# Attention plan of a four-layer decoder: accumulators turned, normalised and put out one step sooner, and x turned closer behind its norm

## The reference, cut to what matters

```
xn  = layernorm(x)
q   = (xn @ Wq + bq) * 8 ** -0.5      # k, v from xn (causal) or from the context (cross)
p   = softmax(q @ k.T + mask/ALiBi)   # 16 heads, 256 x 256
x   = x + (p @ v per head) @ Wo + bo
```

## Time and profile before

| | |
|---|---|
| time, median of 3 runs | 1073.76 us (1073.03 to 1091.79) |
| profiled execution, own time | 1073.34 us |
| its span, first to last instruction | 1071.5 us |
| mean granted TensorE clock | 0.868 of full speed |
| PE, PEld busy | 810.3 us (76%), 590.2 us (55%) |
| DVE, ACT, POOL busy | 613.3 (57%), 349.4 (33%), 316.3 us (30%) |
| the attention of layer 0 in the trace | about 98 to 178 us |
| the attentions of layer 2, the later part beside them | about 448 to 640 us |

### The profile page before, as it was taken

How to read it: one execution, slowest core, us unless ns; L and a number is a source line. 1 busy time by engine, 2 the same in 40 slices (tenths; PEclk the granted TensorE clock), 3 DMA queues, 4 the chain that set the end, 5 groups by cost and what they waited for, 6 DMA issues and landing times. The chain is left out here.

```text
span 1071.5 us, 15970 instructions
## 1 busy us (share of the span) xinstructions
PE 810.3 (76%) x5961; PEld 590.2 (55%) x5969; DVE 613.3 (57%) x1423; ACT 349.4 (33%) x684; POOL 316.3 (30%) x318
## 2 busy tenths in 40 slices
PE   6865896982687285688887747999999995177994
PEld 3632453581354183577654425577877785045994
DVE  4554862323669973885767698663364447742222
ACT  0210574330121112155555623543342331011331
POOL 3263100203238734232222111000251624415232
PEclk9985898896687687899989788999999998558998
DMA  9402200361000005344562000000000000006684
GB/s 362 168 2 87 74 5 1 109 189 27 20 1 1 0 1 106 82 109 87 155 183 60 3 0 1 2 2 2 1 2 2 2 1 1 1 3 211 218 282 145
DMA packets 44966, 72.44 MB, mean 68 GB/s; under 512 B 4849, under 2 KB 37025, under 8 KB 43321
## 3 DMA queue, kind: packets, MB, share of 16 engines
q1 hardware_dynamic: 38921, 65.52, 20.7%
q0 software_dynamic: 1728, 3.59, 1.0%
q10 hardware_dynamic: 4240, 2.30, 0.8%
HBM read 58.65 MB, written 15.89 MB: 70 GB/s over the span
## 5 line engine op out<-in xcount | busy, mean ns | idle before, releaser
L863 DVE TENSOR_REDUCE space<-PS 128x2 f32<-128x512 f32 x128 | 83.8, 686 | 29.3 <-PE PS L667 28.8
L2580 DVE TENSOR_REDUCE space<-PS 128x2 f32<-128x512 f32 x64 | 43.3, 689 | 83.0 <-PE PS L2278 82.8
L847 ACT ACTIVATE annex<-PS 128x384 f32<-128x384 f32 (+1 forms) x128 | 67.2, 544 | 48.5 <-PE PS L678 21.8
L2315 PEld LDWEIGHTS PS<-space 128*128 128x128 f32 x512 | 61.2, 191 | 16.8 <-issue 16.5
L2315 PE MATMUL PS<-space 128*128 128x65 f32 x512 | 68.6, 280 | 0.0
L2295 PE MATMUL PS<-space 64*128 64x256 f32 x256 | 67.0, 402 | 0.2 <-ACT space L2398 0.2
L1982 POOL TENSOR_TENSOR space<-space 128x1536 f32<-128x1536 f32 x16 | 54.6, 3439 | 32.7 <-ACT space L1840 26.4
L2278 PE MATMUL PS<-space 64*128 64x256 f32 x256 | 62.7, 400 | 0.1
L1186 PE MATMUL PS<-space 128*128 128x128 f32 x444 | 55.3, 278 | 6.0 <-ACT space L1255 2.4
L2627 POOL TENSOR_SCALAR var_eps<-moments 128x2 f32<-128x2 f32 x16 | 3.5, 220 | 185.2 <-DVE moments L2409 185.2
L1321 DVE TENSOR_TENSOR space<-PS,space 128x512 f32<-128x512 f32 (+1 forms) x28 | 19.2, 686 | 67.1 <-ACT space L1248 61.9
(11 more groups left out here) (492 smaller groups left out, 2182.8 us busy)
## 6 DMA issues: line engine op xcount, KB each, us to landing
space<-in_e_l_ffn SPq DMA_DIRECT2D x22, 768.0 KB
space<-in_e_l_ffn SPq DMA_DIRECT2D x23, 192.0 KB, 2.6
l_ffn_sorted<-in_slots SPq DMA_DIRECT2D x2, 1584.0 KB, 24.8
space<-l_attn_scratch_k SPq DMA_DIRECT2D x8, 384.0 KB
space<-l_ffn_sorted SPq DMA_DIRECT2D x10, 264.0 KB, 4.2
weights<-in_w_l_xattn SPq DMA_DIRECT2D x1, 2504.0 KB, 13.7
weights<-in_w_l_attn SPq DMA_DIRECT2D x1, 2124.0 KB, 11.8
space<-l_xattn_scratch_q SPq DMA_DIRECT2D x4, 512.0 KB, 3.5
```

The lines of the kernel that those rows point to most:

```text
L847: nc.scalar.activation(P[:, u % 8, 0:keys], PS[:, 3 + u % 2, 0:keys], ACT.Exp).then_inc(exp_done, 1)
L863: nc.vector.tensor_reduce(m[:, :, at_h], max_bank(u).rearrange("p (c k) -> p c k", c=2), AX_X, ALU.max).then_inc(max_done, 1)
L2315: last = nc.tensor.matmul(out, p[:, 256 * kc + 128 * qc:256 * kc + 128 * qc + 128], VB[:, b % 2, kc, h, :], start=kc == 0, stop=kc == 1)
L2580: nc.vector.tensor_reduce(MX[:, b % 2, :, h], PS[:, max_bank[a], :].rearrange("p (c k) -> p c k", c=2), AX_X, ALU.max).then_inc(max_done, 1)
```

## The change

The turn B, the normalisation, the turn E and the output O each move one step ahead. The statistics of x for passes n >= 4 are tied to `out_at`, and so move one step ahead too, and XN with them. The turn of XN moves from two steps behind XN to one step behind for those passes (`lag` is 2 there), and the query with it, so T and Q move two steps. For n < 4 `lag` is 3, and T and Q stay where they are (2 x 3 - 1 = 3 + 2). The copy (L840), K, V and M keep their steps. No instruction is added or removed.

```
--- before.py
+++ after.py
@@ -603,8 +603,8 @@
     done_at = lambda n: second_at(16 * n + 15)
     four_at = {second_at(4 * j + 3) + 2: j for j in range(U // 4)}
     copy_at = {second_at(8 * v + 7) + 3: v for v in range(U // 8)}
-    norm_at = {second_at(8 * v + 7) + 6: v for v in range(U // 8)}
-    out_at = lambda n: done_at(n) + 9
+    norm_at = {second_at(8 * v + 7) + 5: v for v in range(U // 8)}
+    out_at = lambda n: done_at(n) + 8
 
     def norm1_at(n):
         return 9 * n - 20 if n < 2 else first_at(n) - 24 if n < 4 else out_at(n - 4) + 1
@@ -614,8 +614,8 @@
     stats_at, xn_at = {norm1_at(n): n for n in range(N)}, {norm1_at(n) + lag(n): n for n in range(N)}
     jobs = []
     for n in range(N):
-        jobs.append((norm1_at(n) + lag(n) + 2, "T", n))
-        jobs.append((norm1_at(n) + lag(n) + 4, "Q", n))
+        jobs.append((norm1_at(n) + 2 * lag(n) - 1, "T", n))
+        jobs.append((norm1_at(n) + 2 * lag(n) + 1, "Q", n))
         if kind(n) == "causal":
             jobs.append((norm1_at(n) + 6, "K", n))
             jobs.append((norm1_at(n) + 8, "V", n))
@@ -626,7 +626,7 @@
         jobs.append((out_at(n) - 1, "E", n))
         jobs.append((out_at(n), "O", n))
     for v in range(U // 8):
-        jobs.append((second_at(8 * v + 7) + 5, "B", v))
+        jobs.append((second_at(8 * v + 7) + 4, "B", v))
     jobs.sort()
     max_at = {first_at(n) + 19: n for n in range(N)}
     assert all(a[0] < b[0] for a, b in zip(jobs, jobs[2:]))
```

## The result

The changed kernel took 1087.13 us in the median of 4 runs (1084.89 to 1092.70), the kernel before 1074.94 us (4 runs): a ratio of 1.0124, 95% interval 1.0077 to 1.0172. It is slower, by less than 2% and by more than the forecast range allowed. The profiled execution took 1084.89 us, 1083.1 of it the span, 11.6 us more than before. The mean granted clock is 0.868 in both.

The account below looks back on a forecast made before the run. PE was taken to bound the kernel up to about 575 us, then DVE's order. Terms: 9.3 us lost, 6.5 us won, so 1073.34 + 2.8 = 1076.1, forecast 1076 us, range 1069.5 to 1081.

Parts of the forecast that it names:

- The outputs: Layers 0 and 2: O waits 0.35 us less per pass as E's copy starts at once; 2.8 us won.
- slower, but under 2%: Rival, whole program: outputs give nothing back and the first load's 0.6 brings nothing; 6.2 us lost, 1080 us; chance 0.20.
- The 0.5 us forecast as won at 591.38: Late outputs: E's 2.25 us wait for DVE shrinks as its normalisation moves ahead of one maximum; 0.5 us won.
- The turns: Layers 0 and 2: PE waits for the copy of OU at each turn, 0.41 or 0.27 us; 6.7 us lost.
- 2.4 for V: Layer 2 value products: V waits 0.6 us for a normalisation in its bank, four times; 2.4 us lost.
- K and ACT's wait: Layer 2 near 497.81: K comes later and ACT's store wait may move with it; nothing added, bounds 0 and 0.8 us.
- x sooner: Layer 2, later passes: earlier x wins 1.0 us at T and M, and 2.2 us on waits for stacked queries.
- The last normalisation: End of layer 2: it and the last sum go ahead of later work, DVE idles about 1.3 us; 0.2 us lost.
- the rival by the clock: Whole program: 27 added waits each bring a slow stretch of 1.7 us; 46 us lost, about 1120 us; chance 0.02.
- Sum: Whole program: 9.3 us lost against 6.5 us won, so 2.8 us slower, 1076 us.

Follow-up runs that it names:

- outputs_only: Kernel before with only E, O and what hangs on `out_at` (statistics, T and Q of later passes) one step sooner; ratio 1.0118 to the kernel before.
- turns_only: Kernel before with only the turn B and the normalisation one step sooner, in both layers; ratio 1.0116 to the kernel before.
- after_load_later: The whole change, with ACT's load of the turned maxima and its wait for their store two steps later in layer 2; ratio 1.0142 to the kernel before.
- before_load_later: Kernel before with ACT's load of the turned maxima and its wait for their store two steps later in layer 2; ratio 1.0013 to the kernel before.
- e_two_ahead: Kernel before with E two steps ahead of O instead of one, O and M staying; ratio 1.002 to the kernel before.
- after: The changed kernel with the whole change, against the kernel before; median 1087.13 us, ratio 1.0124.
- x_turn_again: Kernel before with only T and Q of the later passes one step sooner in layer 2, a repeat on another chip; ratio 1.0024 to the kernel before.

## Why the prediction was wrong

- **The outputs** are the step that failed: "For three passes of layer 0 and five of layer 2 that is 2.8 us won". Its premise, that the copy starts at once, held. But I priced the output's own wait and not what stood behind it. The kernel before had the last scores of the pass ahead of O; the change put O ahead of them, and the end of the maxima, on which M depends, moved with it. Lost in layer 0: 2.1 us, where 1.05 were forecast as won; by the starts of PE M takes 2.1 us more there, E 0.8 and the second units 0.4, the outputs 0.8 less and the first units 0.4 less. In layer 2 M's delay carried on to a store that lands late among loads, as at 516.52 in outputs_only. My rival "slower, but under 2%" had the outputs give nothing back; that they could cost was in no case, which is one reason why the range ended too low. The 0.5 us forecast as won at 591.38 was not: its wait and the one ahead of it merged, with no change in length.
- **The turns** were right in place and in the wait of the first four (0.41 us). For the next three the whole wait was counted, though they had waited for their copy before, as the earlier trace rows itself shows; in all the turns' waits cost 2.5 us and not 2.9. What was left out is larger: the turn's move also regrouped the steps of scores on ACT, 1.8 us, so that the term is 4.3 us. For layer 2 the forecast was 3.8 us, and 2.4 for V; turns_only has 3.9 to 6.8 us for both together, which fits.
- **K and ACT's wait** at 497.81 did not move with K. It shrank from 3.65 to 1.24 us, outside my 0 to 0.8 us lost. The interval that holds it went from 11.90 to 8.40 us. ACT's waits at 523 (1.69 us) and 548 (2.30 us) made up for it.
- **x sooner**, 3.2 us forecast as won: both waits for queries went, as said, and M was late next, as said. At n = 6 M waits 1.37 us where M and T had 1.66 and 0.73, the 1.0 us of the forecast. But T of the next pass waits 1 us for XN; I had asked only whether its bank was free. What x is worth alone was tested for one of its two steps: nothing that shows.
- **The last normalisation**: DVE idled 1.05 us before the last L906, where I had 1.3; the part behind the attentions took 41.8 against 42.1 us. Right, and small.
- **The clock**: layer 0 kept 1.00 through its turn waits of 0.4 to 0.6 us and two waits of M, 1.10 and 1.33 us (from 130 to 178 us), so short waits cost no clock there. The 2.42 us wait of `four` was followed by 9.2 us at 0.50, which by (1 - 0.50) x 9.2 cost up to 4.6 us; in after_load_later, where PE waits 1.22 us for the turn in that place, the clock stayed at 1.00. The Trainium skill, "TensorE: Matmul & The Clock Gate", Part 1, says that half speed is the default state and activity lifts it. The trace agrees for that long wait, and not for the short ones, nor for one of 2.82 us in before_load_later, which kept 1.00. Over the attentions the change had no lower clock than the kernel before, 0.95 for 0.94, so the rival by the clock was rightly given little, and the clock is not the failed step.
- **Sum**: forecast for layer 0 +1.9 us, measured +6.4, and that is explained in full. For layer 2 the forecast was +0.9, and the attentions are 6.2 to 9.1 us longer (against 147.2 or 144.3). How this divides among turns, outputs and x stays open: turns_only gives 4 to 7 us, outputs_only 13 to 16 with a step of x and up to 8 us of clock in it, one step of x about nothing. They do not add, and the landing of one store among loads, and the clock behind it, change with each.

## What to carry to other kernels

Before a job is moved a step, list what it jumps over, and ask of each whether the end of a chain hangs on it: here the output passed the last scores of a pass, and the maxima, their turn and a store all came later. A wait is worth removing only if the next thing its engine wants is ready; twice here (e_two_ahead, before_load_later) the wait went and others, no shorter in all, came up further on. Where an engine waits in its own queue for a DMA, that DMA's place among larger transfers is part of the schedule: issued 1.7 us ahead of the loads of keys the store of the maxima cost ACT 0.45 us, issued just behind them 4.22. And compare the granted clock of a stage, not its length alone, before a gain or a loss is put down to an edit.

## What the runs showed of the hardware

- The same small store (L820) landed 1.4 us after its issue at the least, 1.7 in the median and 5.3 us at the most in the kernel before; in outputs_only the longest was 6.4 us. The longest, at 492.13, was issued behind loads of stacked keys (490.02 to 491.30), the next, 4.0 us at 554.37, beside saves of keys and a load of weights. That these transfers are what delays it is read from their times and was not tested by itself.
- A wait of 2.82 us at 491.50 in before_load_later left the clock at 1.00 in the 3.5 us behind it; a wait of 2.42 us in after was followed by 9.2 us at 0.50. The length of a single wait does not decide it; how much PE did around it would have to be compared, which was not tried.
- The same instructions with the same waits can get either clock: behind the last copy of layer 0 (L840 to the last L730) after took 3.50 us at 1.00, and after_load_later 4.34 us, at 0.50 for most of it.
- Twelve executions of one program on one core spread over 1066.7 to 1089.1 us (x_turn_again), and four executions of it on another chip had shown 1% that these did not.
